# Projection, edge masks and value tables of a two-layer graph attention as one stage

## The reference

```python
# layer 0
wh = (x @ weight).reshape(n, 8, 64)
awh_i = (wh * linear_i).sum(axis=2)
awh_j = (wh * linear_j).sum(axis=2)
e = leaky_relu(awh_i[:, None, :] + awh_j[None, :, :], negative_slope=0.2)
e = e + ((1.0 - adj) * -1e10)[:, :, None]
out = einsum('ijh,jhf->ihf', softmax(e, axis=1), wh)
x = layernorm(x + out)
# layer 1
adj = maximum(adj, eye)
q, k, v = (einsum('nd,hdk->hnk', x, W) for W in (Wqs, Wks, Wvs))
scores = einsum('hqk,hmk->hqm', q, k) * 64 ** -0.5
scores = scores + 0.01 * eye - 1e16 * (1.0 - adj)
x = layernorm(x + einsum('hqm,hmk,hko->qo', softmax(scores, axis=-1), v, Wo))
```

## Time and profile before

| | |
|---|---|
| time, median of 3 runs | 4451.31 us (4447.39 to 4452.5) |
| the profiled execution, its time | 4445.76 us |
| its span | 4444.0 us |
| mean granted clock of TensorE | 0.934 of full speed |
| busy share: PE, DVE, ACT, POOL | 86%, 79%, 75%, 8% |
| DMA traffic | 691.07 MB, mean 156 GB/s |
| project_gat, first transpose to last projection matmul | 22.49 to 220.4 us |
| build_tables, first adj load issued to the next stage's start | 250.50 to 679.03 us |

### The profile page before, as it was taken

How to read it: one execution, slowest core, us unless ns; L and a number is a source line. 1 busy time by engine, 2 the same in 40 slices (tenths; PEclk the granted TensorE clock), 3 DMA queues, 4 the chain that set the end, 5 groups by cost and what they waited for, 6 DMA issues and landing times. The chain is left out here.

```text
span 4444.0 us, 104687 instructions
## 1 busy us (share of the span) xinstructions
PE 3814.1 (86%) x42884; PEld 2541.4 (57%) x42884; DVE 3499.3 (79%) x6000; ACT 3344.7 (75%) x4172; POOL 356.3 (8%) x559
## 2 busy tenths in 40 slices
PE   7942327999999996992999999999999999999977
PEld 4422227999999993440555555555555555555533
DVE  2155558999999997763888898898889888888734
ACT  1124438999999992220999999999999999999942
POOL 0000000000000000002011120111212011020000
PEclk9965558999999997995999999999999999999999
DMA  2089996555555446765344353544535444353133
GB/s 71 38 275 359 351 342 211 191 183 189 184 184 179 166 150 188 237 208 161 84 124 115 101 143 91 136 113 104 135 100 138 100 119 125 87 155 96 49 107 132
DMA packets 399302, 691.07 MB, mean 156 GB/s; under 512 B 79784, under 2 KB 272488, under 8 KB 361832
## 3 DMA queue, kind: packets, MB, share of 16 engines
q1 hardware_dynamic: 339040, 608.86, 46.0%
q0 software_dynamic: 16512, 58.73, 4.1%
q10 hardware_dynamic: 43280, 16.92, 1.4%
HBM read 532.82 MB, written 151.59 MB: 154 GB/s over the span
## 5 line engine op out<-in xcount | busy, mean ns | idle before, releaser
L1214 DVE CUSTOM_DVE_ANT_0 m_junk<-m_rough,m_rows 128x1024 bf16<-128x1024 f32 x1024 | 1253.3, 1224 | 286.5 <-PE m_rough L1081 225.2
L1163 ACT ACTIVATE m_scores<-m_strip 128x1024 f32<-128x1024 fp8e4 x1024 | 1052.3, 1028 | 102.2 <-POOL m_strip L1012 37.7
L1177 ACT ACTIVATE m_whole<-m_scores 128x1024 int32<-128x1024 f32 x1024 | 1037.9, 1014 | 33.2 <-PE m_scores L1114 22.9
L614 PE MATMUL g_acc<-g_vals,g_pos 128*128 128x130 f16 x8192 | 955.9, 218 | 51.1 <-DVE g_neg L569 51.1
L531 ACT ACTIVATE g_step<-g_arow,k_steep 128x512 fp8e4<-128x512 f32 x1536 | 948.4, 707 | 40.2 <-DVE g_pos L562 37.2
L614 PE MATMUL g_acc<-g_vals,g_neg 128*128 128x130 f16 x8192 | 955.4, 221 | 0.0
L1095 PE MATMUL m_acc<-m_v,m_halves 128*128 128x129 f16 (+1 forms) x16384 | 896.1, 208 | 45.2 <-ACT m_got L1140 45.2
L1095 PEld LDWEIGHTS m_acc<-m_v,m_halves 128*128 128x128 f16 x16384 | 750.1, 98 | 279.5 <-issue 185.9
L614 PEld LDWEIGHTS g_acc<-g_vals,g_pos 128*128 128x128 fp8e4 x8192 | 801.8, 98 | 62.0 <-DVE g_neg L569 37.1
L1109 PE MATMUL m_scores<-m_qA,m_kA 128*128 128x512 f16 x2048 | 780.8, 381 | 5.8 <-ACT m_scores L1163 5.7
L614 PEld LDWEIGHTS g_acc<-g_vals,g_neg 128*128 128x128 fp8e4 x8192 | 784.5, 96 | 0.0
(11 more groups left out here) (153 smaller groups left out, 3089.2 us busy)
## 6 DMA issues: line engine op xcount, KB each, us to landing
g_vals<-scr_gat_v SPq DMA_DIRECT2D x128, 1040.0 KB, 5.2
m_v<-scr_v SPq DMA_DIRECT2D x64, 1032.0 KB, 7.7
b_stage<-in_adj SPq DMA_DIRECT2D x64, 1024.0 KB, 9.2
m_kA<-scr_k_hi SPq DMA_DIRECT2D x128, 512.0 KB, 6.1
scr_row_mask<-b_rowm SPq DMA_DIRECT2D x64, 512.0 KB, 8.6
m_kB<-scr_k_lo SPq DMA_DIRECT2D x64, 512.0 KB, 5.4
m_rows<-scr_row_mask POOLq DMA_DIRECT2D x64, 512.0 KB, 7.3
scr_gat_v<-b_tab SPq DMA_DIRECT2D x32, 520.0 KB, 9.8
```

The costliest lines, as they stand in the source:

```text
L614: mm = pe.matmul(acc[:, b, it, lo:hi], edges[:, n % RING, t, rows], vals[:, b, 4 * j + t, lo:hi], start=j == 0 and t == 0 and lo == 0, sto ...
L1163: nc.scalar.activation(scores[:, n % 2], strip[:, 2 * st:2 * st + 2, :].rearrange("p t i -> p (t i)"), ACT.Copy, bias=-BIG, scale=BIG / ED ...
L1177: nc.scalar.activation(whole[:, st % 2], scores[:, st % 2], ACT.Exp, scale=0.125).then_inc(exped, 1)
L1214: nc.vector.tensor_tensor_reduce(out=junk[:, n % 2], in0=rough[:].rearrange("p a m -> p (a m)"), in1=rows[:, n % TC, n // TC * WIDE:(n // ...
```

## The change

The two stages become one, `front`. Its parts:

- Six edge groups stand beside each of the 8 chunks of the projection. TensorE makes a half group of transposes ("flip", 8 of them) after each tile that it transposes and two after each tile that it projects. VectorE runs two groups ahead of the flips and puts two masks into the transposing part and four beside the projected tiles. ScalarE copies the flips in halves. The remaining groups stand after the chunks: two more masks directly behind them, 12 in the loop over the 32 table tiles (at tiles 1, 4 and 6 of each 8).
- wh stays in SBUF; its store and reload are gone. The maxima are taken tile by tile (tile_top) and chunk by chunk (chunk_topT).
- The loads of x, the store of awh_i, the maxima's round trip and the table stores are issued by POOL; SP has the edge groups and the weights. The ring for adj has 3 buffers instead of 4, x is loaded by tiles into 4 buffers, and the table's two buffers lie where the transposed x and W were.
- The sum over wh stands on TensorE behind the flips of groups 48 and 49 and ahead of those of group 50.

The core of the diff (waits and helpers that are the same in both are left out):

```diff
-def project_gat(nc, k, x, weight, linear_i, linear_j, scr):
-def build_tables(nc, k, adj, scr):
+def front(nc, k, x, adj, weight, linear_i, linear_j, scr):
+    G = C * C
+    EACH = 6
+    AHEAD = 2
+    STAGES = 3
...
-            act.dma_start(scr.wh[:, :, :], wh[:]).then_inc(wh_stored, 16)
...
         @block.sync
         def _(sp):
+            load_group(0)
+            sp.dma_start(w[:], weight.rearrange("(k p) n -> p k n", p=P)).then_inc(loaded_w, 16)
...
+            for g in range(1, STAGES):
+                load_group(g)
+            for g in range(G):
                 sp.wait_ge(masked, g + 1)
                 gate(sp, passed)
+                sp.dma_start(row_v[:, g // C * TC:(g // C + 1) * TC, g % C, :], rowm[:, g % 2]).then_inc(row_out[g % 2], 16)
+                if g + STAGES < G:
+                    load_group(g + STAGES)
+                if g > 0:
+                    store_col(g - 1)
+            store_col(G - 1)
...
+        @block.gpsimd
+        def _(pool):
+            def load_x(n):
+                if n >= TC:
+                    pool.wait_ge(t_done, n - TC + 1)
+                pool.dma_start(xs[:, n % TC, :], x_v[:, n, :]).then_inc(x_in[n % TC], 16)
...
+            pool.wait_ge(topped, 2)
+            pool.dma_start(scr.top_a[:, :], topT[:]).then_inc(top_out, 16)
+            pool.dma_start(scr.top_wh[:, :], top[:]).then_inc(top_out, 16)
+            pool.wait_ge(top_out, 32)
...
+            for t in range(NT):
+                pool.wait_ge(low, 2 * (t + 1))
+                pool.dma_start(scr.gat_v[:, :, t, :].rearrange("h p v -> p h v"),
+                               tab[:, t % 2].rearrange("p h z v -> p h (z v)")).then_inc(tab_out[t % 2], 16)
...
+            def project(n):
...
+                if n > 0:
+                    pe.wait_ge(wh_copied, 2 * n)
...
+            def flip(n):
+                g, half = n // 2, n % 2
+                pe.wait_ge(edged, g + 1)
+                if n >= 2:
+                    pe.wait_ge(copied, n - 1)
+                for jt in range(2):
+                    for it in range(TC):
+                        mm = pe.transpose(flipped[:, half, jt * CW + it * P:jt * CW + (it + 1) * P],
+                                          edge[:, g % 2, it, (2 * half + jt) * P:(2 * half + jt + 1) * P], k.identb[:])
+                mm.then_inc(flip_done, 1)
+
+            for c in range(C):
+                for t in range(TC):
+                    turn(TC * c + t)
+                    flip(2 * EACH * c + t)
+                for t in range(TC):
+                    project(TC * c + t)
+                    flip(2 * EACH * c + TC + 2 * t)
+                    flip(2 * EACH * c + TC + 2 * t + 1)
+                across(c)
+            for n in range(2 * EACH * C, 2 * (EACH * C + AHEAD)):
+                flip(n)
+            pe.wait_ge(wh_copied, 2 * NT)
+            for t in range(NT):
+                mm = pe.matmul(ps_wh[:, 0, :], k.ones[:], wh[:, t, :], start=t == 0, stop=t == NT - 1)
+            mm.then_inc(sum_done, 1)
+            for n in range(2 * (EACH * C + AHEAD), 2 * G):
+                flip(n)
...
+            def mask(g):
+                dve.wait_ge(adj_in[g % STAGES], 16 * (g // STAGES + 1))
+                if g >= 2:
+                    dve.wait_ge(flip_done, 2 * g - 2)
+                nc.vector.tensor_scalar(edge[:, g % 2], stage[:, g % STAGES], EDGE, None, ALU.mult).then_inc(edged, 1)
+                if g >= 2:
+                    dve.wait_ge(row_out[g % 2], 16 * (g // 2))
+                nc.vector.tensor_scalar(rowm[:, g % 2], stage[:, g % STAGES], BIG, -BIG, ALU.mult, ALU.add).then_inc(masked, 1)
...
+            mask(0)
+            dve.wait_ge(loaded_w, 48)
...
+            mask(1)
+            for c in range(C):
+                g = EACH * c + AHEAD
+                copy_turned(TC * c)
+                copy_turned(TC * c + 1)
+                mask(g)
+                copy_turned(TC * c + 2)
+                copy_turned(TC * c + 3)
+                mask(g + 1)
+                for t in range(TC):
+                    ins = top_of(TC * c + t)
+                    mask(g + 2 + t)
+                copy_across(c)
...
+            for t in range(NT):
...
+                if t % 8 in (1, 4, 6):
+                    mask(g)
+                    g += 1
...
+            for n in range(2 * EACH * C, 2 * (EACH * C + 2 * AHEAD)):
+                copy_flipped(n)
+            act.wait_ge(ready, 1)
             nc.scalar.activation(vf[:, 0], shift[:], ACT.Exp).then_inc(exped, 1)
...
+            for t in range(NT):
+                b = t % 2
+                if t >= 2:
+                    act.wait_ge(tab_out[b], 16 * (t // 2))
...
+                if t % 8 in (2, 5, 7):
+                    copy_flipped(n)
+                    copy_flipped(n + 1)
+                    n += 2
```

More of the change, by code:

```diff
@@ L149, in project_gat @@
[L149 to L172, removed]
@@ L293, in build_tables, with load_group @@
         col_v = scr.edge_T.rearrange("(t p) (g j) -> p t g j", p=P, j=CW)
[L294 removed]
         @block.sync
         def _(sp):
[L298 to L306 removed]
+            def load_group(g):
+                sp.dma_start(stage[:, g % STAGES], adj_v[:, g // C * TC:(g // C + 1) * TC, g % C, :]).then_inc(adj_in[g % STAGES], 16)
@@ L327, in groups @@
-            def groups(i, more):
-                for b in range(4):
-                    store_group(4 * i + b, b)
-                    if more:
-                        load_group(4 * i + b + 4, b)
-            for i in range(0, NT // 2 - 1):
-                groups(i, True)
-                for b in range(2):
-                    sp.wait_ge(mult, 2 * (2 * i + b + 1))
-                    gate(sp, passed)
-                    sp.dma_start(wh[:, b, :], scr.wh[:, ds(2 * i + b + 2, 1), :].rearrange("p a d -> p (a d)")).then_inc(ld[b], 16)
-                    store(i, b)
@@ L399, in _, with copy_flipped @@
+            assert g == G
+            dve.wait_ge(sum_done, 1)
+            nc.vector.tensor_scalar(k.mean_wh[:], ps_wh[:, 0, :], 1.0 / N, None, ALU.mult)
         @block.scalar
         def _(act):
-            act.sem_inc(col_out[0], 16)
-            act.sem_inc(col_out[1], 16)
-            act.sem_inc(stored[0], 16)
-            act.sem_inc(stored[1], 16)
-            act.wait_ge(chain, 4)
+            def copy_flipped(n):
+                g, half = n // 2, n % 2
+                act.wait_ge(flip_done, n + 1)
+                if half == 0 and g >= 2:
+                    act.wait_ge(col_out[g % 2], 16 * (g // 2))
+                nc.scalar.copy(colm[:, g % 2, 2 * half:2 * half + 2, :].rearrange("p t i -> p (t i)"), flipped[:, half],
+                               saturate=False).then_inc(copied, 1)
@@ new lines, in copy_wh @@
+            def copy_wh(n):
+                act.wait_ge(wh_done, n + 1)
+                nc.scalar.copy(wh[:, n, :], ps_wh[:, n % 2, :]).then_inc(wh_copied, 1)
+                nc.scalar.copy(aij[:, n, :], ps_a[:, 0:2 * H]).then_inc(wh_copied, 1)
+            for c in range(C):
+                for t in range(TC):
+                    copy_flipped(2 * EACH * c + t)
+                for t in range(TC):
+                    copy_wh(TC * c + t)
+                    copy_flipped(2 * EACH * c + TC + 2 * t)
+                    copy_flipped(2 * EACH * c + TC + 2 * t + 1)
```

330 lines of the change are left out of this document (136 added, 194 removed).

## The result

The changed kernel takes **4263.6 us**, the median of 4 runs (4260.6 to 4264.4), against 4449.8 of the kernel before in the same series (4447.4 to 4452.5). The ratio is 0.958, with a 95% interval of 0.9564 to 0.9597. I had forecast 4269 us and faster. The profiled execution took 4264.1 us with a span of 4260.6, and the attention starts at 491.3 us, where the prediction had 497.

The account below looks back on a forecast made before the run. Before, TensorE bound the projection and DMA the tables; merged, 24.5 + 276 + 39 + 152 + 5.5 = 497 us against 679 takes 182 us from 4445.8, leaving 4263.8; with 5.5 us to the median, 4269 us. Range 4218 to 4345.

Parts of the forecast that it names:

- Start: Before the chunks: first projection matmul at about 31.4 us, chunks counted from 24.5 us.
- The chunks: Eight projection chunks, each beside six edge groups: 34.5 us a chunk, bounds 33.4 and 40, ending at 300.5 us.
- the lower bound of 33.4: Time in us of a chunk on TensorE's chain, with DMA wholly hidden.
- The turning part: A chunk's transposes of x with copies and a VectorE mask: 3.7 + 2.4 + 0.8 = 6.9 us.
- Between: From the last chunk to the first table: 39 us, lower bound 36, with the loop starting at 339.5 us.
- The loop: 32 table tiles and 12 groups: (2.5 + L)/2 = 4.75 us a tile, 152 us; bounds 139 or 120, and 197.
- POOL's queue: Table stores meeting VectorE's masks: 12 of 32 land 2.5 us later, 15 us more, a loop of 167 us.
- The sum: Front's terms in us: 24.5 + 276 + 39 + 152 + 5.5 = 497, where the attention starts, against 679.
- the forecast's own third limit: In the table loop, a table buffer is free again only when its store has landed: (2.5 + L)/2 us a tile.
- The rivals that made more of it: Table stores land late: L 9.8, 4314 us (chance 0.28 with late edge queue); two buffers throttle loop: 4584 (0.04).
- L: Landing time of a table store in the loop, taken as 7 us.
- One sign of being wrong: In the table loop: a table store taking over 10 us to land would show the prediction wrong.

Follow-up runs that it names:

- experiments 5 to 8: Four variants of the changed kernel: copies before the mask (4258.4 us), x loaded once (4261.4), both (4253.6), x loaded twice (4275.9).
- experiment 3: Changed kernel with the sum over wh behind the flips of groups 50 and 51 instead of ahead of them: 4250.9 us.
- Experiment 1: Changed kernel with four table buffers instead of two, nothing else: 4227.0 us.
- experiment 4: Changed kernel with the table loop's mask behind the low halves instead of between products and low halves: 4259.3 us.
- Experiment 2: Changed kernel with the table stores issued on SP's queue instead of POOL's: 4264.3 us.
- Experiment 12: Changed kernel with four table buffers, flips of groups 50 and 51 first, three additions of the wh sum behind each loop group: 4215.7 us.
- experiment 9: Changed kernel with four table buffers, wh sum behind the flips of groups 50 and 51, and all four copies before the mask: 4243.8 us.
- experiment 10: As experiment 9, against the changed kernel, with four groups instead of two ahead of the table loop and ten in it: 4238.7 us.
- experiment 5: Changed kernel with all four copies of a turning part ahead of the chunk's first mask: 4258.4 us.

## Why the prediction was right, and where it was not

**Start.** "About 31.4 us" for the first projection matmul was 34.3. The products of the weights begin at 15.6 us in place of 10.3: the last of the weights' loads lands 5 us later, with 1 MB of edges ahead and x beside it, where I had counted 1.8. It cost little, since from that matmul to its end the first chunk took 25.3 us, where the prediction's 34.5 - 6.9 gives 27.6. It ends at 59.7; the prediction's 24.5 + 34.5 gives 59.0.

**The chunks.** This is the term that was sized too dear: 34.5 us were taken, 30.7 measured, seven times 3.8 = 26.5 us. Even the lower bound of 33.4 was too high. The turning part is 6.1 us (243.2 to 249.3) instead of 6.9. A tile with its group is 5.25 us apart (249.29, 254.53, ...) instead of 5.72: the transposes cost 0.9 us and not 1.07, and the 0.3 us for each semaphore did not come on top. The transposed product is 3.61 us as in the earlier trace rows. 6.1 + 4 x 5.25 + 3.6 = 30.7. On DMA's side 31.6 us at 382 GB/s became 30.8 at 392. That the two would be within 2 us was right, and experiments 5 to 8 put it at 0.2. Of the 3.8 us, 0.8 are the turning part and 1.9 the four tiles, and 1.1 are what I had added to the 33.4 for a row mask that lands late. No row gave that last part its size, and it isn't there: VectorE waited only 1.8 us in all for row masks. The clock stayed at 1.00.

**Between.** 39 us forecast, 37.3 measured, by the order that was read from the code; experiment 3 moved it by 8.8 us.

**The loop.** 152 us forecast, 174 measured; this is the step that failed on the other side. The form, (chain + landing)/2 a tile, holds. From the timeline's issues the time from a free buffer to POOL's issue is 3.4 us on average where I had taken 2.5. I had priced the tile without a mask, although 12 of 32 tiles have one between products and low halves. At places 1 and 4 of each eight tiles, counted from 0, it stands in the chain, and that takes 4.5 to 5.8 us; at place 6 VectorE does it while ScalarE still waits for the buffer, and the chain is 2.6 to 3.0 us. The other tiles take 2.6 to 4.1 us. From the issue to the next use of the buffer it is 7.7 us on average instead of 7.0, a mean of the short and the long landings told above and not a landing on a half loaded DMA. Together 11.1 us, half of it for each of 31 tiles, is 172 us. Experiment 1 shows the cause by removing it, experiment 4 that moving the mask inside the circle does not shorten it.

**POOL's queue.** The Trainium skill, SBUF — State Buffer, section "SBUF: two separate sides", led me to an estimate of 167 us, nearer to 174 than my 152. Experiment 2 takes the stores off POOL's queue, and the loop still lasts 173 us. So that estimate was near for a reason that isn't there, and weighing the rule lower was right for these stores. An effect of its kind is in this case's traces, but small: where experiment 4 lets the mask run beside the store's issue, the issue takes 0.4 us more, not 2.5, and in the changed kernel, where the issue stands ahead of the next mask, it is 0.89 us (0.93 at most).

**The sum.** +0.7 (first chunk), -26.5, -1.7, +22.0, -0.1 is -5.6 us, and the attention starts 5.7 us earlier than forecast. In the whole kernel the profiled execution took 4264.1 us for a predicted 4263.8: the 4 us behind the front and some 2 us outside the span filled up the rest, and both are scatter. The range would have held with either error alone (about 4241 and 4291 us); that the time came within 6 us of 4269 is what the two signs gave. The pair of table buffers, the forecast's own third limit, is what bound the loop. The rivals that made more of it had its size wrong: L is 7.7 us on average and not 9.8, let alone 18. One sign of being wrong did show in part: single table stores took over 10 us to land, 11.9 at most, though the median was 6.9.

**What stays open.** Experiment 12's loop has DMA shares above 1.0 at only 277 to 287 GB/s, against 392 in the chunks. The table stores, in rows of 520 bytes, are in that loop and not in the chunks, which speaks for them as the cause; another layout of the tables was not tried. From 320 to 400 us of experiment 12 POOL's queue, which carries the tables, moved 10.13 MB in 50.9% of the 16 engines' time, which would be 249 GB/s at a full share, and SP's queue with the edge groups 12.38 MB in 53.3%, 290 GB/s; in the chunks SP's queue moved 76.81 MB in 99.6% of 213 us, 362 GB/s. So the groups' transfers had become dearer too, and the table stores' own packets don't account for all of it. Nor was it tried why ScalarE waits so much longer for experiment 9's column stores than for experiment 10's (30.8 us against 20.0).

## What to carry to other kernels

Before two stages are merged, price each chain that goes round through a buffer as (work + wait for landing)/buffers, with every instruction that stands in it in order, those of the other stage too. One more pair of buffers was worth 37 us here. A long reduction that nobody waits for does not belong in one piece in front of short work on an in-order engine: moved as a whole it found a new victim once the loop was fast (experiments 9 and 10), cut into pieces its cost vanished (12). Where two limits are as near to each other as here (0.2 of 30.7 us), an edit of one of them shows next to nothing, and it takes a run that moves both to see it. A mean share of 0.80 can hide a DMA that is full in bursts, and then a landing is not the one of a partly loaded DMA but now a short and now a long one.

## What the hardware showed that I had not expected

*POOL's issues are slow beside VectorE's masks.* Its loads of x in the chunks, in the changed kernel and then in experiment 5 (groups of POOL from 59 to 262 us):

```profile
L220 POOL DMA_DIRECT2D a_xs<-in_x x24 | 40.1, 1679 | 0.0
```

```profile
L220 POOL DMA_DIRECT2D a_xs<-in_x x24 | 12.9, 542 | 4.3 <-PE a_turned L254 4.2
```

The instruction is the same. In the changed kernel the four loads of a chunk are issued while VectorE does its masks (SBUF to SBUF, f32 to bf16), in experiment 5 while it does the copies out of PSUM, and one issue takes 1,679 ns against 542, 2,949 at most. The rule of the Trainium skill, SBUF — State Buffer, section "SBUF: two separate sides", that POOL cannot write descriptors while VectorE holds two ports, fits this. Here it is the issue that grows, by up to 2.4 us, and no landing (5.7 to 8.3 us in the changed kernel, 4.9 to 9.0 in experiment 5). Experiment 4 shows the same for the table stores' issue, at 0.4 us, and there the mask grows as well. It costs this kernel nothing, as each load has nearly a chunk of time.

*One core drew 392 GB/s over 213 us*, from and to memory together, with loads of 1 MB and 256 KB and stores of 512 and 256 KB mixed; before, the best stretch read was 382.

*TensorE's clock stayed at 1.00 in the chunks and fell to 0.50 (1.2 GHz) in the loop*, where it does 12 groups' flips. With the sum spread over the loop (experiment 12) TensorE was busy 18.5 and 19.8 of 40 us, where experiment 1 has 20.8 of 120, and the granted clock was 0.74.
